# Stacked q and k loaded by six transfers on 48, 32 and 16 partitions instead of twelve on 16

## The chip, the cores and the metric

The kernel runs on one core of a Trainium2 chip. The metric is the device time of one execution in microseconds, lower is better. The core has a matrix engine (TensorE, PE in the profile, with PEld for its weight loads), VectorE (DVE), ScalarE (ACT), GpSimd (POOL) and SyncE (SP), which here only issues transfers between DRAM and the on-chip memory (SBUF, 128 partitions). Sixteen DMA engines carry the transfers. The result must equal the reference in float32.

## The reference

A transformer block of six sublayers on 4 x 1024 tokens of 256 features; attention occurs twice, after a mixture-of-experts sublayer and after a table-lookup sublayer:

```python
x = x + 0.5 * _L0_ffn_ref(_layernorm(x), ...)
x = x + _L0_attn_ref(_layernorm(x), Wq, bq, Wk, bk, Wv, bv, Wo, bo)
x = x + 0.5 * _L0_ffn_ref(_layernorm(x), ...)
x = x + 0.5 * _L1_ffn_ref(_layernorm(x), ...)
x = x + _L1_attn_ref(_layernorm(x), Wq, Wk, Wv, Wp)
x = x + 0.5 * _L1_ffn_ref(_layernorm(x), ...)
```

Both attentions have 16 heads of dimension 16, causal:

```python
q = (jnp.einsum('btc,oc->bto', x, Wq) + bq).reshape(Bb, Tt, H, D).transpose(0, 2, 1, 3)
logits = jnp.einsum('bhqd,bhkd->bhqk', q, k) / jnp.sqrt(jnp.float32(D))
attn = jax.nn.softmax(jnp.where(causal, -jnp.inf, logits), axis=-1)
out = jnp.einsum('bhqk,bhkd->bhqd', attn, v).transpose(0, 2, 1, 3).reshape(Bb, Tt, C)
y = jnp.einsum('btc,oc->bto', out, Wo) + bo
```

## The kernel before, in words

The phases run one after the other: moe0, attn0, moe1, lut0, attn1, lut1. An attention phase is a projection (`project_phase`) followed by the heads stage (`heads_phase`).

**Projection.** The weights are loaded into `w_raw` and split into a rounded part `w_hi` (ACT, L453) and a rest `w_lo` (DVE, L567), since float32 products are made of three products of rounded operands. In attn0 the biases of q and k come into `b_col` by two loads (L256), and `bv_row` by one behind them (L258); ACT waits for all of them (`b_loaded`, 48) ahead of its read of the indices of the lookup. For each tile of 512 tokens, q and k come out with their 256 features on partitions, in two halves of 128 rows. Each value is then split into three bfloat16 parts, which are stored to `q_dram` and `k_dram`, of shape (batch 4, part 3, feature 256, token 1024) in bfloat16. Row h x 16 + d of a part is dimension d of head h.

**Heads.** The stage goes over 16 quads, n = 4 x batch + quad, of four heads each. For a quad, q and k stand in `q_st` and `k_st` as stacks on 96 partitions: six blocks of 16 dimensions, with 4 heads x 1024 tokens in the free dimension, 8 KB per partition. The blocks pair the parts of q and k so that one matmul over 96 partitions sums the six products (0,0), (1,0), (2,0), (0,1), (1,1), (0,2) of parts. There are R = 3 such stacks, used in turn.

For each quad, PE computes 32 units of scores (L1008), whose row maxima DVE takes (L1180). GpSimd splits the maxima in three parts, PE turns them (L1018), DVE copies them out, and SP writes them into three more rows of the stack, 96 to 98 (`put_max`, L847, from 96 partitions to 3). Then PE computes the scores transposed over 99 rows (L1027, 48 pieces in a quad, `st_full`), ACT takes their exponential (L1118), and PE multiplies with v (L1043). PE runs the units ahead: in quad n it interleaves the units of quad n+1 from the tenth on and the first nine of quad n+2 (LEAD = 9, by the list PACE). The first unit of a quad waits for its stack's twelve transfers (`stack_loaded`, LOAD).

**SP's order around the loads.** At the start: load(0), load(1), the output weights, the bias, load(2), put_max(0). Then for each n from 0 to 15: for 1 <= n < 14 wait until the transposed scores of quad n-1 are done (`st_full`) and issue load(n+2); store(n-1, 1) and store(n, 0) of o (L843); put_max(n+1); for n = 0 three loads of x (L878); and `output_ahead(n)`, which in the first quad of a batch loads the sums and rows of the batch before (L857, L860) and x, and in the second stores the inverses (L864) and loads them spread over 16 dimensions each (`load_inv`, L872, source (8 heads, 16 repeated, 512) onto 128 partitions). All of these are transfers on one queue. `load` is L829 to L838:

```python
for at, (ql, kl) in enumerate(((0, 0), (1, 0), (2, 0), (0, 1), (1, 1), (0, 2))):
    to = slice(at * HD, (at + 1) * HD)
    sp.dma_start(q_st[to, r, :, :], q_v[ql]).then_inc(stack_loaded[r], 16)
    sp.dma_start(k_st[to, r, :, :], k_v[kl]).then_inc(stack_loaded[r], 16)
```

A view `q_v[l]` is (16 dimensions, 4 heads, 1024 tokens) with runs of 2 KB in DRAM, since the rows of one dimension of neighbouring heads lie 16 rows apart.

Of the kernel before, what the change touches and what calls it, by code (L numbers as in the profile page):

```python
# [5 lines left out]
ALU = mybir.AluOpType  # L6
ACT = mybir.ActivationFunctionType
AX = mybir.AxisListType
F32 = mybir.dt.float32
# [4 lines left out]
P = 128  # L14
TOK = 4096
D = 256
KD = D // P
# [15 lines left out]
HEADS = 16  # L33
HD = D // HEADS
SEQ = 1024
# [4 lines left out]
QUAD = P // VW  # L40
QUADS = HEADS // QUAD
SPLIT = 3
# [46 lines left out]
def project_phase(nc, name, x_in, w_qkv, b_qkv, q_dram, k_dram, v_sb, consts, combine=None, lookup=None):  # L89
# [6 lines left out]
    with ExitStack() as ctx:  # L96
        def sb(n, shape, dt=F32):
            return ctx.enter_context(nc.sbuf_tensor(f"{name}_{n}", shape, dt))
# [6 lines left out]
        def sem(n):  # L105
            sems.append(ctx.enter_context(nc.semaphore(f"{name}_{n}")))
            return sems[-1]

        w_raw = sb("w_raw", [P, 3, KD, D])
        w_hi = sb("w_hi", [P, 3, KD, D], F32R)  # L110
        w_lo = sb("w_lo", [P, 3, KD, D], F32R)
# [13 lines left out]
        if biased:  # L125
            b_col = sb("b_col", [P, 4])
# [11 lines left out]
        b_loaded = sem("b_loaded")  # L138
        w_hi_ready = sem("w_hi_ready")
# [64 lines left out]
        def x_complete(engine, t):  # L204
            engine.wait_ge(x_loaded[t % RX], 16 * (t // RX + 1))
            if combine:
                engine.wait_ge(y_used, SUB * (t + 1))

        def idx_slot(c):
            return 1 if c == CHUNKS - 1 else 0  # L210

        with nc.Block() as block:

            @block.sync
            def _(sp):
                def load_x(t):
                    if t >= RX:
                        if combine:
                            sp.wait_ge(x_stored[t % RX], 16 * (t // RX))
                        sp.wait_ge(xn_ready, t - RX + 1)  # L220
                    sp.dma_start(x_sb[:, t % RX, :, :], x_in_v[t, :, :, :]).then_inc(x_loaded[t % RX], 16)

                def load_idx(c):
                    slot = idx_int[:, idx_slot(c), :]
                    loaded = idx_loaded[idx_slot(c)]
                    gate_up = slot[:, 0:2 * D].rearrange("p (m k h) -> p m k h", m=2, k=KD)
                    if c < CHUNKS - 1:
                        if c >= 1:
                            sp.wait_ge(idx_ready, c)
                        for m in range(2):  # L230
                            sp.dma_start(gate_up[:, m, :, :], idx[m].rearrange("(k p) h -> p k h", p=P)[:, :, c * P:(c + 1) * P])\
                                .then_inc(loaded, 16)
                        sp.dma_start(slot[:, 2 * D:3 * D], idx[2][c * P:(c + 1) * P, :]).then_inc(loaded, 16)
                    else:

                        sp.wait_ge(idx_padded, 1)
                        for m in range(2):
                            sp.dma_start(gate_up[:, 0, :, m * HALF:m * HALF + TAIL],
                                         idx[m].rearrange("(k p) h -> p k h", p=P)[:, :, c * P:INTER]).then_inc(loaded, 16)
                        sp.dma_start(slot[HALF:HALF + TAIL, 2 * D:3 * D], idx[2][c * P:INTER, :]).then_inc(loaded, 16)  # L240

                def store_found(piece):
                    sp.wait_ge(found_ready, piece + 1)
                    sp.dma_start(w_dram[:, piece * TILE:(piece + 1) * TILE], found[:, piece % 2, :]).then_inc(found_stored[piece % 2], 16)

                load_x(0)
                for n, w in enumerate(w_qkv):
                    sp.dma_start(w_raw[:, n, :, :], w.rearrange("(k p) o -> p k o", p=P)).then_inc(w_loaded, 16)
                if lookup:
                    sp.dma_start(lut_row[:, :], lut.rearrange("(a n) -> a n", a=1).to_broadcast([P, LUT])).then_inc(lut_loaded, 16)  # L250
                    load_idx(0)
                for t in range(1, RX):
                    load_x(t)
                if biased:
                    for n in range(2):
                        sp.dma_start(b_col[:, 2 * n:2 * n + 2], b_qkv[n].rearrange("(m p) -> p m", p=P),  # L256
                                     allow_slow_non_contiguous=True).then_inc(b_loaded, 16)
                    sp.dma_start(bv_row[:, :], b_qkv[2].rearrange("(a d) -> a d", a=1)).then_inc(b_loaded, 16)  # L258
                if lookup:
                    load_idx(CHUNKS - 1)  # L260
                    for c in range(1, CHUNKS - 1):
                        load_idx(c)
                for t in range(TILES):
                    if combine:
                        x_complete(sp, t)
                        sp.dma_start(x_out_v[t, :, :, :], x_sb[:, t % RX, :, :]).then_inc(x_stored[t % RX], 16)
                    if lookup:
                        store_found(t)
                    for m in range(4):
                        dram = (q_dram, k_dram)[m // 2]  # L270
                        rows = slice((m % 2) * P, (m % 2 + 1) * P)
                        sp.wait_ge(parts_ready, t * 4 + m + 1)
                        sp.dma_start(dram[t // 2, :, rows, (t % 2) * TILE:(t % 2 + 1) * TILE].rearrange("l r t -> r l t"),
                                     parts[:, t % 2, m, :, :]).then_inc(qk_stored[t % 2], 16)
                        if m == 0 and t + RX < TILES:
                            load_x(t + RX)
                if lookup:
                    for piece in range(TILES, PIECES):
                        store_found(piece)
                    for r in range(2):  # L280
                        sp.wait_ge(found_stored[r], 16 * len(range(r, PIECES, 2)))
                if combine:
                    for r in range(RX):
                        sp.wait_ge(x_stored[r], 16 * len(range(r, TILES, RX)))
                for r in range(2):
                    sp.wait_ge(qk_stored[r], 64 * (TILES // 2))
# [118 lines left out]
            def _(act):  # L405
# [44 lines left out]

                for n in range(3):
                    act.wait_ge(w_loaded, 48)
                    act.activation(w_hi[:, n, :, :], w_raw[:, n, :, :], ACT.Copy).then_inc(w_hi_ready, 1)  # L453
                if biased:
                    act.wait_ge(b_loaded, 48)
                    act.activation(bv_parts[:, 0, :], bv_row[:, :], ACT.Copy).then_inc(bv_hi_ready, 1)
                if lookup:
                    for c in range(CHUNKS):
# [36 lines left out]
            def _(dve):  # L495
# [68 lines left out]
                                          ALU.mult).then_inc(diag_ready, 1)  # L564
                for n in range(3):
                    dve.wait_ge(w_hi_ready, n + 1)
                    dve.tensor_tensor(w_lo[:, n, :, :], w_raw[:, n, :, :], w_hi[:, n, :, :].bitcast(F32), ALU.subtract)\  # L567
                        .then_inc(w_ready, 1)
                for half in range(2):
                    if lookup:  # L570
# [117 lines left out]
def heads_phase(nc, name, q_dram, k_dram, v_sb, o_dram, inv_dram, x_in, x_out, w_o, b_o, consts):  # L688
# [10 lines left out]
    NR = 4  # L699
    DEPTH = 6 * HD  # L700
    ROWS = DEPTH + SPLIT
    LOAD = 12 * 16
    SB, OB = 4, 1
    UNIT_AT, TURN_AT = score_banks(NQ, SB)
    DIAGONAL = [s for s, (half, j) in enumerate(STEPS) if j * P >= half * TILE]
# [21 lines left out]
    with ExitStack() as ctx:  # L727
# [12 lines left out]
        q_st = sb("q_st", [P, R, QUAD, SEQ], BF16)  # L740
        k_st = sb("k_st", [P, R, QUAD, SEQ], BF16)
# [8 lines left out]
        w_raw = sb("w_raw", [P, KD, D])  # L750
        w_hi = sb("w_hi", [P, KD, D], F32R)
        w_lo = sb("w_lo", [P, KD, D], F32R)
# [12 lines left out]
        stack_loaded = [sem(f"stack_loaded{r}") for r in range(R)]  # L765
# [15 lines left out]
        b_loaded = sem("b_loaded")  # L781
        w_hi_ready = sem("w_hi_ready")
# [42 lines left out]
        with nc.Block() as block:  # L825

            @block.sync
            def _(sp):
                def load(n):  # L829
                    b, quad = divmod(n, QUADS)  # L830
                    r = n % R
                    rows = slice(quad * QUAD * HD, (quad + 1) * QUAD * HD)
                    q_v = [q_dram[b, l, rows, :].rearrange("(h d) t -> d h t", d=HD) for l in range(SPLIT)]
                    k_v = [k_dram[b, l, rows, :].rearrange("(h d) t -> d h t", d=HD) for l in range(SPLIT)]
                    for at, (ql, kl) in enumerate(((0, 0), (1, 0), (2, 0), (0, 1), (1, 1), (0, 2))):
                        to = slice(at * HD, (at + 1) * HD)
                        sp.dma_start(q_st[to, r, :, :], q_v[ql]).then_inc(stack_loaded[r], 16)
                        sp.dma_start(k_st[to, r, :, :], k_v[kl]).then_inc(stack_loaded[r], 16)  # L838

                def store(n, half):  # L840
                    b, quad = divmod(n, QUADS)
# [155 lines left out]
            def _(pe):  # L997
                def unit(g):
# [3 lines left out]
                    if k == 0:  # L1002
                        pe.wait_ge(stack_loaded[r], LOAD * (n // R + 1))
                    if over:
# [1550 lines left out]
```

## Time and profile before

| | us |
|---|---|
| median of 3 runs | 2983.54 |
| lowest, highest | 2978.67, 2984.82 |
| the profiled execution | 2974.38 |
| its span | 2972.6 |
| heads stage of attn0 | about 748 to 1303 |
| heads stage of attn1 | about 2178 to 2726 |

The rows further down come from the one profiled execution. PE, DVE, ACT, POOL and SP are the engines; SPq is SyncE's own queue of instructions, in which a transfer's row is its issue, not its movement. L1008 is line 1008 of the kernel. The granted clock (PEclk) is a share of TensorE's full speed of 2.4 GHz; the lower level is 1.2 GHz. A DMA share is the mean busy share of the 16 DMA engines, so one engine is 0.06. Every transfer leaves, beside its packets of data, small packets that signal its completion.

### The profile page before, as it was taken

The page shows a single profiled execution, that of the slowest core. Times are in us where ns is not written, and L with a number is a line of the kernel's source. Part 1 is how long each engine was busy: PE and PEld are TensorE (multiplying, and loading weights), DVE is VectorE, ACT ScalarE, POOL GpSimd, SP SyncE. Part 2 cuts the span into 40 slices and gives each one's busy share as a digit, 9 for nine tenths or more (in the row PEclk, how much of TensorE's full clock was granted, in tenths as well). Part 3 has the DMA queues.
Part 4 walks back from the last instruction along what each step waited for, and adds up shares of the span by engine and source line. Part 5 has one row for each costly group of instructions (what it writes and reads, how often), then busy time and mean ns, then how long its engine had stood idle before and what let it go on. Part 6 is the DMA issues. An engine that isn't in the chain of part 4 may idle for free. (4 is left out here: it accounts for less than half of the span.)

```text
span 2972.6 us, 49393 instructions
## 1 busy us (share of the span) xinstructions
PE 2472.1 (83%) x15186; PEld 1598.4 (54%) x15186; DVE 1951.5 (66%) x5464; ACT 1459.7 (49%) x3374; POOL 1131.3 (38%) x1578
## 2 busy tenths in 40 slices
PE   7965995788699889859929984996869999984998
PEld 6755994455133323348719973774623333333776
DVE  6854885576688768458728864773658877843444
ACT  3433552333277768624405542433627877772433
POOL 4774444665232222217754436650122222220000
PEclk9987997899699999979969996998969999997999
DMA  4453554454665666144435544331574656524000
GB/s 133 171 145 128 178 180 152 152 180 147 79 104 96 83 103 108 61 143 148 170 104 176 179 151 138 112 96 54 162 111 83 98 91 117 90 59 156 29 29 29
DMA packets 266560, 351.35 MB, mean 118 GB/s; under 512 B 41873, under 2 KB 196034, under 8 KB 266306
## 3 DMA queue, kind: packets, MB, share of 16 engines
q1 hardware_dynamic: 226370, 239.08, 35.2%
q0 software_dynamic: 39936, 109.11, 10.8%
q8 instruction: 132, 2.16, 0.3%
q14 instruction: 122, 1.00, 0.1%
HBM read 197.32 MB, written 149.95 MB: 117 GB/s over the span
## 5 line engine op out<-in xcount | busy, mean ns | idle before, releaser
L1180 DVE CUSTOM_DVE_ANT_0 attn_heads_masked_s<-attn_heads_s_ps,attn_heads_causal 128x768 bf16<-128x768 f32 (+7 forms) x1024 | 727.6, 754 | 214.5 <-PE attn_heads_s_ps L1008 212.8
L1118 ACT ACTIVATE attn_heads_probs<-attn_heads_st_ps 128x512 f32<-128x512 f32 (+3 forms) x1536 | 662.9, 494 | 270.2 <-PE attn_heads_st_ps L1027 256.9
L1008 PE MATMUL attn_heads_s_ps<-attn_heads_k_st,attn_heads_q_st 96*128 96x512 bf16 (+3 forms) x1536 | 410.3, 348 | 92.4 <-DMA attn_heads_k_st<-k_dram 77.7
L1027 PE MATMUL attn_heads_st_ps<-attn_heads_q_st,attn_heads_k_st 99*128 99x512 bf16 (+3 forms) x1536 | 427.2, 337 | 4.3 <-ACT attn_heads_probs L1118 3.6
L1043 PE MATMUL attn_heads_o_ps<-attn_heads_probs,attn_v_sb 128*32 128x512 f32 (+3 forms) x3072 | 335.0, 509 | 2.9 <-POOL attn_heads_probs L958 2.3
L1027 PEld LDWEIGHTS attn_heads_st_ps<-attn_heads_q_st,attn_heads_k_st 99*128 99x128 bf16 x1536 | 136.9, 98 | 350.7 <-ACT attn_heads_probs L1118 251.8
L958 POOL TENSOR_SCALAR_AFFINE_SELECT attn_heads_probs<-attn_heads_probs 128x512 f32<-128x512 f32 x256 | 163.7, 640 | 404.8 <-ACT attn_heads_probs L1118 399.7
L1463 POOL DMA_INDIRECT xs_dram<-moe_route_xn,rows_at x256 | 272.6, 1065 | 79.0 <-issue 76.4
L1008 PEld LDWEIGHTS attn_heads_s_ps<-attn_heads_k_st,attn_heads_q_st 96*128 96x128 bf16 x1536 | 137.2, 101 | 218.5 <-DMA attn_heads_k_st<-k_dram 83.0
L1958 POOL DMA_DIRECT2D ys_dram<-moe_expert_y_sb x288 | 158.0, 549 | 243.6 <-DVE moe_expert_y_sb L2076 243.6
L2032 ACT ACTIVATE moe_expert_xT_hi<-moe_expert_xT_ps 128x256 fp32r<-128x256 f32 x288 | 110.9, 385 | 196.2 <-PE moe_expert_xT_ps L1976 195.9
L1976 PE MATMUL moe_expert_xT_ps<-ident,moe_expert_x_sb 128*128 128x128 f32 x576 | 113.3, 279 | 98.6 <-DMA moe_expert_x_sb<-xs_dram 95.8
L2058 DVE TENSOR_TENSOR moe_expert_xT_lo<-moe_expert_xT_ps,moe_expert_xT_hi 128x256 fp32r<-128x256 f32 x288 | 122.3, 425 | 111.0 <-ACT moe_expert_xT_hi L2032 107.5
L1990 PE MATMUL moe_expert_gu_ps<-moe_w_hi,moe_expert_xT_hi 128*128 x576 | 189.0, 328 | 2.1 <-DVE moe_expert_xT_lo L2058 2.1
L1990 PE MATMUL moe_expert_gu_ps<-moe_w_hi,moe_expert_xT_lo 128*128 x576 | 163.7, 284 | 0.0
L1990 PE MATMUL moe_expert_gu_ps<-moe_w_lo,moe_expert_xT_hi 128*128 x576 | 163.5, 284 | 0.0
L70 POOL DMA_INDIRECT lut_y_sb<-ys_dram,rows_at x128 | 133.3, 1041 | 66.3 <-issue 36.1
L70 POOL DMA_INDIRECT attn_proj_y_sb<-ys_dram,rows_at x128 | 135.2, 1056 | 50.8 <-issue 37.1
L2341 ACT ACTIVATE lut_gate<-lut_g_ps 128x512 f32<-128x512 f32 x96 | 57.3, 597 | 194.2 <-PE lut_g_ps L2252 194.1
L2419 DVE SCALAR_TENSOR_TENSOR lut_hid<-lut_gate,lut_u_ps 128x512 f32<-128x512 f32 x80 | 54.9, 687 | 137.0 <-PE lut_u_ps L2252 132.8
L946 POOL CAST attn_heads_max_parts<-attn_heads_row_max 128x32 bf16<-128x32 f32 x32 | 6.8, 211 | 340.4 <-DVE attn_heads_row_max L1180 340.4
L368 PE MATMUL attn_proj_w_ps<-attn_proj_mask,attn_proj_diag 128*128 128x512 bf16 x432 | 109.9, 414 | 31.6 <-DVE attn_proj_mask L542 26.2
(263 smaller groups left out, 5941.8 us busy)
## 6 DMA issues: line engine op xcount, KB each, us to landing
moe_expert_x_sb<-xs_dram SPq DMA_DIRECT2D x288, 128.0 KB, 2.1
ys_dram<-moe_expert_y_sb POOLq DMA_DIRECT2D x288, 128.0 KB, 2.1
attn_heads_q_st<-q_dram SPq DMA_DIRECT2D x192, 128.0 KB, 8.7
attn_heads_k_st<-k_dram SPq DMA_DIRECT2D x192, 128.0 KB, 9.1
o_dram<-attn_heads_oT SPq DMA_DIRECT2D x64, 256.0 KB, 5.8
moe_route_w_raw<-in_L_ffn_we_dram SPq DMA_DIRECT2D x96, 128.0 KB
q_dram<-attn_proj_parts SPq DMA_DIRECT2D x32, 384.0 KB, 2.9
k_dram<-attn_proj_parts SPq DMA_DIRECT2D x32, 384.0 KB, 3.1
```

The costliest lines, as they stand in the source:

```text
L70: pool.indirect_dma_start(y_sb[:, r, k, :], None, ys_dram, bass.IndirectOffsetOnAxis(rows_at[:, u, k:k + 1], 0))\
L958: pool.affine_select(out=d, in_=d, compare_op=ALU.is_ge, fill=0.0, base=0, pattern=[[0, QUAD], [1, P]], channel_multiplier=-1).then_inc(ma ...
L1008: last = pe.matmul(s_ps[:, at + a // TILE, 0:w], q_st[0:DEPTH, r, h, i * P:(i + 1) * P], k_st[0:DEPTH, r, h, a:a + w], start=True, stop=True)
L1027: pe.matmul(st_ps[:, v % NB, 0:w], k_st[0:ROWS, n % R, h, j * P:(j + 1) * P], q_st[0:ROWS, n % R, h, first:first + w], start=True, stop=Tr ...
L1043: last = pe.matmul(o_ps[h * VW:(h + 1) * VW, use % OB, TILE - w:TILE], v_sb[:, at:at + VW], probs[:, G % NR, h, 0:w], start=(j == 0), stop ...
L1118: act.activation(probs[:, G % NR, h, 0:w], st_ps[:, v % NB, 0:w], ACT.Exp, scale=scale)\
L1180: dve.tensor_tensor_reduce(out=masked_s[:, use % 4, 0:w], in0=s_banks[:, at * TILE:at * TILE + w], in1=causal[:, SEQ - w:SEQ], scale=1.0, ...
L1463: pool.indirect_dma_start(xs_dram, bass.IndirectOffsetOnAxis(rows_at[:, n * SUB + s, k:k + 1], 0), xn[:, n % RX, s, :], None).then_inc(sca ...
L1958: pool.dma_start(ys_dram[s * P:(s + 1) * P, :], y_sb[:, s % AHEAD, :]).then_inc(y_stored[s % AHEAD], 16)
L1976: last = pe.transpose(xT_ps[:, s % 2, kd * P:(kd + 1) * P], x_sb[:, s % AHEAD, kd * P:(kd + 1) * P], ident[:, :])
L1990: last = pe.matmul(gu_ps[:, s % 2, 0:D], a, b, start=(n == 0), stop=(n == len(pairs) - 1))
L2058: dve.tensor_tensor(xT_lo[:, s % RH, :, :].rearrange("p k t -> p (k t)"), xT_ps[:, s % 2, 0:D], xT_hi[:, s % RH, :, :].rearrange("p k t -> ...
```

## The change

The rows of q and k are stored in another order. Within each half of 128 rows, row d x 8 + h is now dimension d of the h-th head of that half. To this end, the rounding of wq and wk reads the columns in that order and writes them side by side, the rest likewise, and the biases of q and k come by four loads of 128 values instead of two of 256. Wv keeps its order.

In DRAM one dimension of the four heads of a quad is then one run of 8 KB. The load of a stack is made of three transfers each for q and k: for l = 0, 1, 2 the blocks of 16 partitions that pair part l of k with parts 0 to 2 - l of q are loaded at once. The q transfer takes its 3, 2 or 1 parts from DRAM, the k transfer repeats part l 3, 2 or 1 times. They go to 48, 32 and 16 partitions. The bytes written into SBUF and the stack that results are as before but for the order of q's and k's columns, which is the same for both.

```diff
+        def in_order(w, n):
+            return w[:, n, :, :].rearrange("p k (m d h) -> p (k m) d h", d=HD, h=HEADS // KD) if n < 2 else w[:, n, :, :]
+
+        def by_dim(w, n):
+
+            return w[:, n, :, :].rearrange("p k (m h d) -> p (k m) d h", d=HD, h=HEADS // KD) if n < 2 else w[:, n, :, :]
...
-                        sp.dma_start(b_col[:, 2 * n:2 * n + 2], b_qkv[n].rearrange("(m p) -> p m", p=P),
-                                     allow_slow_non_contiguous=True).then_inc(b_loaded, 16)
+                        for m in range(KD):
+                            some = b_qkv[n][m * P:(m + 1) * P].rearrange("(h d) -> d h", d=HD)
+                            sp.dma_start(b_col[:, 2 * n + m:2 * n + m + 1], some, allow_slow_non_contiguous=True).then_inc(b_loaded, 16)
...
-                    act.activation(w_hi[:, n, :, :], w_raw[:, n, :, :], ACT.Copy).then_inc(w_hi_ready, 1)
+                    act.activation(in_order(w_hi, n), by_dim(w_raw, n), ACT.Copy).then_inc(w_hi_ready, 1)
                 if biased:
-                    act.wait_ge(b_loaded, 48)
+                    act.wait_ge(b_loaded, 80)
...
-                    dve.tensor_tensor(w_lo[:, n, :, :], w_raw[:, n, :, :], w_hi[:, n, :, :].bitcast(F32), ALU.subtract)\
+                    dve.tensor_tensor(in_order(w_lo, n), by_dim(w_raw, n), in_order(w_hi, n).bitcast(F32), ALU.subtract)\
...
-    LOAD = 12 * 16
+    LOAD = 2 * SPLIT * 16
...
-                    rows = slice(quad * QUAD * HD, (quad + 1) * QUAD * HD)
-                    q_v = [q_dram[b, l, rows, :].rearrange("(h d) t -> d h t", d=HD) for l in range(SPLIT)]
-                    k_v = [k_dram[b, l, rows, :].rearrange("(h d) t -> d h t", d=HD) for l in range(SPLIT)]
-                    for at, (ql, kl) in enumerate(((0, 0), (1, 0), (2, 0), (0, 1), (1, 1), (0, 2))):
-                        to = slice(at * HD, (at + 1) * HD)
-                        sp.dma_start(q_st[to, r, :, :], q_v[ql]).then_inc(stack_loaded[r], 16)
-                        sp.dma_start(k_st[to, r, :, :], k_v[kl]).then_inc(stack_loaded[r], 16)
+                    rows = slice(quad // 2 * P, (quad // 2 + 1) * P)
+                    q_v, k_v = (x[b, :, rows, :].rearrange("l (d q h) t -> l d q (h t)", d=HD, h=QUAD)[:, :, quad % 2, :] for x in (q_dram, k_dram))
+                    for l in range(SPLIT):
+                        at, count = sum(SPLIT - m for m in range(l)), SPLIT - l
+                        to = slice(at * HD, (at + count) * HD)
+                        sp.dma_start(q_st[to, r, :, :], q_v[0:count]).then_inc(stack_loaded[r], 16)
+                        sp.dma_start(k_st[to, r, :, :], k_v[l:l + 1].to_broadcast([count, HD, QUAD * SEQ])).then_inc(stack_loaded[r], 16)
```

## Rows read from the trace of the kernel before

**Rows 1.** The page: busy time by engine, with share of the span and instructions.

```profile
PE 2472.1 (83%) x15186; PEld 1598.4 (54%) x15186; DVE 1951.5 (66%) x5464; ACT 1459.7 (49%) x3374; POOL 1131.3 (38%) x1578
```

**Rows 2.** Busy time by stretch, quads 4 and 6 of attn0; columns on top.

```profile
core 0: us, PE busy (x) PEld busy (x) DVE busy (x) ACT busy (x) POOL busy (x), PEclk, DMA share, GB/s
898.00:925.00 27.00, 27.00 (x201) 9.53 (x193) 23.26 (x66) 21.73 (x51) 6.01 (x12) 1.00 0.55 80
952.00:989.00 37.00, 29.35 (x197) 10.06 (x193) 23.20 (x67) 21.94 (x52) 8.44 (x14) 0.86 0.63 88
```

**Rows 3.** Timeline of PE, attn0: start, us, engine, line, operation, [idle before, releaser].

```profile
763.49 1.36 PE L1008 MATMUL attn_heads_s_ps<-attn_heads_k_st,attn_heads_q_st 96*128 96x512 bf16 x4 [20.17 <-DMA attn_heads_k_st<-k_dram]
794.85 1.49 PE L1027 MATMUL attn_heads_st_ps<-attn_heads_q_st,attn_heads_k_st 99*128 99x512 bf16 x3
...
983.18 0.82 PE L1008 MATMUL attn_heads_s_ps<-attn_heads_k_st,attn_heads_q_st 96*128 96x512 bf16 x2 [7.65 <-DMA attn_heads_k_st<-k_dram]
1074.03 0.81 PE L1008 MATMUL attn_heads_s_ps<-attn_heads_k_st,attn_heads_q_st 96*128 96x512 bf16 x2 [4.48 <-DMA attn_heads_k_st<-k_dram]
```

**Rows 4.** Waits, whole span: us in total, times, longest.

```profile
PE attn_heads_s_ps L1008 <- DMA attn_heads_k_st<-k_dram: 77.7, 12, 20.4
```

**Rows 5.** DMA from 748 to 763 us, first loads: packets, MB, share of 16 engines.

```profile
q1 hardware_dynamic: 1077, 1.78, 101.1%
```

**Rows 6.** DMA from 1203 to 1215 us, 40 slices: four inv_all loads, one store.

```profile
DMA  0000233555455556445555311000000069500000
GB/s 0 0 0 0 27 68 143 198 198 212 191 198 212 198 178 191 184 184 198 205 205 205 150 75 48 27 0 0 0 0 0 0 273 410 191 0 0 0 0 0
DMA packets 688, 1.31 MB, mean 109 GB/s; under 512 B 48, under 2 KB 48, under 8 KB 688
q1 hardware_dynamic: 688, 1.31, 29.6%
```

**Rows 7.** Timeline of SP's queue: issues of loads, of put_max (L847) and load_inv (L872).

```profile
748.13 0.34 SPq L837 DMA_DIRECT2D attn_heads_q_st<-q_dram  x1
...
822.86 0.32 SPq L837 DMA_DIRECT2D attn_heads_q_st<-q_dram  x1
...
955.13 2.45 SPq L872 DMA_DIRECT2D attn_heads_inv_all<-inv_dram  x4
957.63 0.46 SPq L837 DMA_DIRECT2D attn_heads_q_st<-q_dram  x1
...
994.17 0.32 SPq L837 DMA_DIRECT2D attn_heads_q_st<-q_dram  x1
...
1084.69 0.46 SPq L837 DMA_DIRECT2D attn_heads_q_st<-q_dram  x1
...
1164.88 0.73 SPq L847 DMA_DIRECT2D attn_heads_q_st<-attn_heads_turned  x1
1170.64 0.50 SPq L837 DMA_DIRECT2D attn_heads_q_st<-q_dram  x1
1200.05 0.80 SPq L847 DMA_DIRECT2D attn_heads_q_st<-attn_heads_turned  x1
...
2251.77 0.32 SPq L837 DMA_DIRECT2D attn_heads_q_st<-q_dram  x1
...
2620.84 0.80 SPq L847 DMA_DIRECT2D attn_heads_q_st<-attn_heads_turned  x1
```

**Rows 8.** DMA from 898 to 901 us, 40 slices: one put_max alone.

```profile
DMA  0000000000000000001222221000000000000000
DMA packets 99, 0.02 MB, mean 8 GB/s; under 512 B 99, under 2 KB 99, under 8 KB 99
```

**Rows 9.** DMA issues, whole span: count, KB each, median us to landing.

```profile
attn_heads_sums<-o_dram SPq DMA_DIRECT2D x16, 32.0 KB, 2.2
```

**Rows 10.** Line 453: ns min/median/max, first and last start, forms.

```profile
L453 ACT ACTIVATE attn_proj_w_hi<-attn_proj_w_raw x6: 612/613/629, 485.5 to 2063.2; 128x512 fp32r<-128x512 f32 x6
```

**Rows 11.** Timeline of SP's queue, projection of attn0: the first bias load.

```profile
483.92 1.54 SPq L256 DMA_DIRECT2D attn_proj_b_col<-in_L_attn_bq_dram  x1
```

## The prediction

> **What bounds the kernel now.** The page comes first: PE is the busiest engine over the span, DVE next [rows 1]. The chain that ended last says nothing here: it covers the last stage (lut) and stops there. So the busy time by stretch is next. In an undisturbed quad of the heads stage PE is busy 27.00 of 27 us at the full clock; in quad 6 it is busy 29.35 of 37 us, at a granted clock of 0.86 [rows 2]. PE is the bound of a normal quad, and something else stops it in some. The timeline of PE names it: the first score matmul of a quad waits for the load of the stacks, 20.17 us at the start of the stage, then 7.65 and 4.48 us [rows 3]; over both attentions it is 12 waits, 77.7 us [rows 4]. The loads are therefore on the path already, at the edge: what makes a load shorter removes up to those 77.7 us and the slow clock behind them, and what makes it longer than now stalls every quad.
>
> The DMA answer for the first 15 us of the stage shows what a load costs. The 16 engines are busy the whole time (101.1%) and yet move only 1.78 MB, 119 GB/s [rows 5]. All 16 engines write into the same 16 partitions there. Where 16 engines write 128 partitions, a 256 KB store reaches 410 GB/s [rows 6]. The Trainium skill explains this ("SBUF — State Buffer", section "Door 1: The DMA port swizzle (why [64,N] ≈ [32,N])"): partitions reach memory through 16 ports, and 16 neighbours lie on four. The low rate in the rows agrees.
>
> **What the change does to a load.** A load stays at 12 x 128 KB = 1.573 MB. Six transfers of 384, 256 and 128 KB take the place of twelve; a run in a partition is 8 KB instead of 2 KB. SP issues six instructions fewer, 0.32 to 0.46 us each [rows 7]; that is up to 2.8 us of SP per load, but not on the path, since the engines were the limit at 119 GB/s [rows 5]. I cost it at nothing; were the engines no limit it would give at most 2.8 us a load.
>
> The decisive question is how many engines a transfer uses. Before, the outermost dimension of a load is 16 on both sides. After, the source of the 48-partition transfer is (3, 16, 4096), that of the 32-partition one (2, 16, 4096), for q over the part and for k a repeat. Two transfers of this trace have such a small outer dimension. The load of inv_all has source (8, 16, 512) with the 16 a repeat and a destination of 128 partitions: four loads and one store give 688 packets, 640 of data and 48 under 512 B. The store on 16 engines accounts for 16 of the 48, so the loads leave 8 each; and they hold half of the engines busy (slices of 4 to 5 tenths) [rows 6]. The maxima go from 96 partitions into 3: 99 packets, 96 of data and three more, with 2 tenths busy, that is 3 of 16 engines [rows 8]. So the small outer dimension of either side sets the number of engines: the new transfers should run on 3, 2 and 16 engines.
>
> The Trainium skill has the same as a rule, and it speaks against this change ("DMA: Bandwidth & Descriptors", "Why a DMA increments its semaphore by 16 and not by 1"): the count is the largest up to 16 that divides the slowest dimension of both sides, and a leading repeat of c copies confines the transfer to c engines. Both rows agree with it. By it alone the result is the same as by the rows.
>
> **Length of a load after.** Taking the engines in order, the first carries 16 partitions x 8 KB of each of the four large transfers and one partition of each of the two small ones: 66 x 8192 B = 540.7 KB, out of 1.573 MB; 13 engines carry 16 KB each. Its rate: in [rows 6] 1.31 MB took 29.6% of 16 engines over 12 us, 56.8 engine-us, so 23.1 KB per us; the store's best slice gives 410/16 = 25.6. I take 23.1, since those loads too run on part of the engines and write SBUF: 540.7/23.1 = 23.4 us. Issue and landing add about 2.1 (a 32 KB transfer lands after 2.2 us [rows 9]): a load takes 25.5 us. With 25.6 it is 23.2; for 8 KB pieces no row exists, and I go down to 20 KB per us, 29.1 us.
>
> **What that costs in a quad.** SP issues load(n+2) when quad n begins. PE first needs it about 18 us later: issue at 957.63, PE stalled from 975.53 (983.18 less 7.65) [rows 3, 7]. From the end of the stall to the next load's issue it took 11.0 and 10.7 us (983.18 to 994.17, 1074.03 to 1084.69) [rows 3, 7], mean 10.9; that holds the rest of the quad with the slow clock that follows a stall, and the put_max transfer, which lands after the load. So the period after is 25.5 + 10.9 = 36.4 us, in every quad with a load, 13 per attention. Five of these loads are issued right behind others: inv_all is issued from 955.13 on, its four parts put 4 x 32 KB on each of the first eight engines, 5.7 us at 23.1, so until about 962, where the load would have started at 958.6; 3.2 us more [rows 7]. I take 3.2 for all five (two with inv_all, three with rows, of which two with x, 2 to 4 us): 16. Sum: 13 x 36.4 + 16 = 489.2 us per attention.
>
> Before, the same 13 periods took in the first attention 1170.64 - 822.86 = 347.8 plus 35.2 for the last (put_max 1164.88 to 1200.05) = 383.0. In the second, from the same load's issue to the same put_max 2620.84 - 2251.77 = 369.1, and put_max comes 5.8 ahead of the quad's load (1164.88, 1170.64): 374.9 [rows 7]. Added: 106.2 and 114.3.
>
> At the start, three loads stand in the queue, then put_max(0) behind them, on the same three engines. 748.1 + 2.1 + 3 x 23.4 + 1.4 (output weights, bias, the maxima) = 821.8, where the first transposed scores ran at 794.85 [rows 3]: +27 us, twice. The first units begin 10 us later (25.5 instead of 15.4 after the issue), inside that 27: their 31.1 us to 794.6 would end at 804.7. Quad 0 itself (794.85 to 822.86) stays.
>
> **Small parts.** The rounding of wq and wk reads with a stride of 64 B: 613 ns on ACT per matrix [rows 10], at the start of the projection. Bounds 0 to double, four matrices: 0 to 2.5 us on ACT, and as much again on DVE behind it; I take 0, it writes the same elements once. The q and k biases come by four loads instead of two, the first of which took 1.54 us on SP [rows 11], and bv_row is issued behind them, with ACT waiting for it and the index reads behind ACT: -0.5 to +3 us, I take 1. The stores of q and k, the matmuls, the masks stay.
>
> **Sum.** 106.2 + 114.3 + 54 + 1 = 275.5. The profiled execution took 2974.4 us; 3249.9. The median of the runs shown is 9.1 above it: 3259 us.
>
> **Rivals.** (A) Faster: the outer dimension doesn't confine these transfers and all 16 engines share them. What decides is whether 48 destination partitions are split by 16, against [rows 6, 8]. Then the partitions count: 119 GB/s on 16 [rows 5], 410 on 128 [rows 6]; between them I estimate twice 119 for both 32 and 48. 2 x (1.6 + 1.1 + 1.1) = 7.6 us for 384, 256 and 128 KB instead of 13.2. A load 5.6 us shorter leaves 2.1 of the 7.65 stall and next to nothing of the others; of the 77.7 us of waits 40.6 stand at the two starts (20.2 each, [rows 3, 4]), so 37 are in quads, and about 33 go, with the slow clock behind them (a quad of 37 us against 27 for 7.65 us of stall [rows 2, 3]) about 50, and 11 at the starts: 2983.5 - 61 = 2923. (The Trainium skill's port map, section as above, puts partitions 32 to 47 on the ports of the first 16, which would make the 48-partition transfer 1.5 times as fast as one on 16, not twice.)
>
> (B) Much slower: the first and third engine write partitions 0 to 15 and 32 to 47 in step and disturb each other. For it: sixteen engines on 16 partitions are limited to 119 GB/s in all [rows 5]. Against it: eight engines at once, in blocks of 16 partitions, keep 184 to 212 GB/s, 23 to 26 each [rows 6]. Price: q and k of the 48-partition transfer put 128 KB on each engine, 5.6 us at 23.1; at half that rate all the time +11.2 us, half of the time +5.6; I take the mean, 8.4. It adds in full, since a load is already past the 18 us. Each us of load costs 13 + 3 per attention, 32 in all: +269, 3528. (The skill's port map gives this rival its reason: partitions p and p + 32 lie on one port.)
>
> (C) No effect: a load is hidden anyway. The 12 waits [rows 4] exclude it unless both changes cancel.
>
> **Chances.** Forecast 0.68, own range 3175 to 3385 (rate 25.6: -2.3 us, -74; 20: +3.6, +115). B 0.22, 3435 to 3620. A 0.08, 2900 to 2960. C 0.02. Range 3175 to 3620 leaves out A, C and the ends of the others, about 0.18. A difference within 0.2% can't be told from none: faster 0.08, same 0.01, slower 0.91 (C counts half as small loss).
>
> **What the profile after would show.** Load transfers with 51, 34 and 32 packets if pieces are 8 KB (48+3, 32+2, 16+16); DMA share near 3 tenths in the large ones, and a long tail with 2; landing near 25 us. PE waiting for the load in every quad from the second on, 6 to 8 us, a granted clock near 0.85 to 0.9, periods of 36 to 37. If the slices show 9 tenths or a load lands within 12 us, A holds; if landing is 32 or more, B. Periods of 36 with another cause of the wait (put_max, o_dram) would make the mechanism wrong though the time be right.

## The result and the profile after

| | before | after |
|---|---|---|
| median, us | 2982.18 (4 runs) | 3324.43 (4 runs) |
| lowest to highest | 2978.67 to 2984.82 | 3317.73 to 3330.85 |
| span of the profiled execution | 2972.6 | 3316.0 |
| heads stage of attn0, from the first load's issue to the next phase's | 748.1 to 1303.0: 554.9 | 747.1 to 1472.1: 725.0 |
| heads stage of attn1 | 2178.1 to 2726.3: 548.1 | 2347.4 to 3069.5: 722.1 |

The ratio is 1.1148, with a 95% interval of 1.1123 to 1.1174. The two heads stages account for 344.1 of the 343.4 us by which the span grew. The forecast was 3259 us, range 3175 to 3620.

The busy time of the page answers to [rows 1]. PE's busy time grew by 44 us only; its share fell from 83% to 76%.

```profile
span 3316.0 us, 49187 instructions
PE 2516.1 (76%) x15170; PEld 1604.9 (48%) x15186; DVE 1953.9 (59%) x5464; ACT 1462.9 (44%) x3374; POOL 1130.8 (34%) x1578
```

The waits over the whole span answer to [rows 4]: 28 waits and 351.6 us instead of 12 and 77.7. PE waits at both starts and in each of the 26 quads with a load.

```profile
PE attn_heads_s_ps L1016 <- DMA attn_heads_k_st<-k_dram: 351.6, 28, 34.4
```

The timeline of PE answers to [rows 3]; columns as there. The first row is the start of the stage, the second the first transposed scores, which now wait for the maxima's transfer. Then come two undisturbed quads, one behind the rows of o, one behind inv_all.

```profile
776.40 1.35 PE L1016 MATMUL attn_heads_s_ps<-attn_heads_k_st,attn_heads_q_st 96*128 96x512 bf16 x4 [34.12 <-DMA attn_heads_k_st<-k_dram]
820.37 1.44 PE L1035 MATMUL attn_heads_st_ps<-attn_heads_q_st,attn_heads_k_st 99*128 99x512 bf16 x3 [12.42 <-DMA attn_heads_q_st<-attn_heads_turned]
...
914.72 0.82 PE L1016 MATMUL attn_heads_s_ps<-attn_heads_k_st,attn_heads_q_st 96*128 96x512 bf16 x2 [9.43 <-DMA attn_heads_k_st<-k_dram]
950.95 0.82 PE L1016 MATMUL attn_heads_s_ps<-attn_heads_k_st,attn_heads_q_st 96*128 96x512 bf16 x2 [7.36 <-DMA attn_heads_k_st<-k_dram]
...
1034.14 0.82 PE L1016 MATMUL attn_heads_s_ps<-attn_heads_k_st,attn_heads_q_st 96*128 96x512 bf16 x2 [14.89 <-DMA attn_heads_k_st<-k_dram]
1077.86 0.82 PE L1016 MATMUL attn_heads_s_ps<-attn_heads_k_st,attn_heads_q_st 96*128 96x512 bf16 x2 [14.83 <-DMA attn_heads_k_st<-k_dram]
```

SP's queue, the issues of the loads that end those waits, and the two of put_max that close the sum of the periods; answers to [rows 7]:

```profile
747.09 0.84 SPq L845 DMA_DIRECT2D attn_heads_q_st<-q_dram  x1
...
848.33 0.74 SPq L845 DMA_DIRECT2D attn_heads_q_st<-q_dram  x1
886.82 0.73 SPq L845 DMA_DIRECT2D attn_heads_q_st<-q_dram  x1
925.12 0.72 SPq L845 DMA_DIRECT2D attn_heads_q_st<-q_dram  x1
...
1000.54 0.74 SPq L845 DMA_DIRECT2D attn_heads_q_st<-q_dram  x1
1045.16 0.75 SPq L845 DMA_DIRECT2D attn_heads_q_st<-q_dram  x1
...
1323.03 0.77 SPq L855 DMA_DIRECT2D attn_heads_q_st<-attn_heads_turned  x1
1328.78 0.76 SPq L845 DMA_DIRECT2D attn_heads_q_st<-q_dram  x1
1367.31 0.77 SPq L855 DMA_DIRECT2D attn_heads_q_st<-attn_heads_turned  x1
```

A load is issued at 886.82 and PE goes on at 914.72: 27.9 us. For the next shown it is 25.8 (925.12 to 950.95). Behind the rows it is 33.6, behind inv_all 32.7. The DMA answer for the second of these loads, 925 to 951 us in 40 slices of 0.65 us, beside [rows 5]:

```profile
DMA  0030218921174222212111211119111111111111
GB/s 0 0 38 13 76 50 252 177 25 50 50 284 170 88 60 91 76 76 88 76 76 76 88 76 72 66 66 378 73 38 50 50 63 50 50 50 50 50 41 47
DMA packets 515, 2.11 MB, mean 81 GB/s; under 512 B 72, under 2 KB 72, under 8 KB 320
```

Some 4 us after the issue, for somewhat over 1 us, nearly all 16 engines work (8 and 9 tenths), on the two small transfers, which were issued last; a store of o passes at 284 and another at 378 GB/s. Otherwise the rate is mostly 60 to 91 GB/s with 1 or 2 tenths busy (3 of 16 engines) and in the end about 50 GB/s with 1 tenth (2 of 16).

### The profile page after: what moved, and what is told of

It is laid out like the page before. It is cut to its first block and busy times, and to the rows that moved or that the text cites. A ratio compares the mean times of both kernels' runs of the same rounds, so it can differ in the third digit from the quotient of the medians.

```text
span 3316.0 us, 49187 instructions
## 1 busy us (share of the span) xinstructions
PE 2516.1 (76%) x15170; PEld 1604.9 (48%) x15186; DVE 1953.9 (59%) x5464; ACT 1462.9 (44%) x3374; POOL 1130.8 (34%) x1578
## 5 line engine op out<-in xcount | busy, mean ns | idle before, releaser
L1188 DVE CUSTOM_DVE_ANT_0 attn_heads_masked_s<-attn_heads_s_ps,attn_heads_causal 128x768 bf16<-128x768 f32 (+7 forms) x1024 | 729.8, 755 | 553.8 <-PE attn_heads_s_ps L1016 551.6
L1016 PE MATMUL attn_heads_s_ps<-attn_heads_k_st,attn_heads_q_st 96*128 96x512 bf16 (+3 forms) x1536 | 424.0, 358 | 366.4 <-DMA attn_heads_k_st<-k_dram 351.6
L1035 PE MATMUL attn_heads_st_ps<-attn_heads_q_st,attn_heads_k_st 99*128 99x512 bf16 (+3 forms) x1536 | 441.1, 347 | 30.5 <-DMA attn_heads_q_st<-attn_heads_turned 26.4
L966 POOL TENSOR_SCALAR_AFFINE_SELECT attn_heads_probs<-attn_heads_probs 128x512 f32<-128x512 f32 x256 | 163.1, 637 | 726.8 <-ACT attn_heads_probs L1126 722.1
L1051 PE MATMUL attn_heads_o_ps<-attn_heads_probs,attn_v_sb 128*32 128x512 f32 (+3 forms) x3072 | 352.4, 533 | 0.7 <-ACT attn_heads_oT L1107 0.5
L70 POOL DMA_INDIRECT lut_y_sb<-ys_dram,rows_at x128 | 133.8, 1045 | 66.5 <-issue 36.1
```

The lines of the kernel that those rows point to most:

```text
L70: pool.indirect_dma_start(y_sb[:, r, k, :], None, ys_dram, bass.IndirectOffsetOnAxis(rows_at[:, u, k:k + 1], 0))\
L966: pool.affine_select(out=d, in_=d, compare_op=ALU.is_ge, fill=0.0, base=0, pattern=[[0, QUAD], [1, P]], channel_multiplier=-1).then_inc(ma ...
L1016: last = pe.matmul(s_ps[:, at + a // TILE, 0:w], q_st[0:DEPTH, r, h, i * P:(i + 1) * P], k_st[0:DEPTH, r, h, a:a + w], start=True, stop=True)
L1035: pe.matmul(st_ps[:, v % NB, 0:w], k_st[0:ROWS, n % R, h, j * P:(j + 1) * P], q_st[0:ROWS, n % R, h, first:first + w], start=True, stop=Tr ...
L1051: last = pe.matmul(o_ps[h * VW:(h + 1) * VW, use % OB, TILE - w:TILE], v_sb[:, at:at + VW], probs[:, G % NR, h, 0:w], start=(j == 0), stop ...
L1188: dve.tensor_tensor_reduce(out=masked_s[:, use % 4, 0:w], in0=s_banks[:, at * TILE:at * TILE + w], in1=causal[:, SEQ - w:SEQ], scale=1.0, ...
```

## Experiments

The experiments ran in three groups, each on another chip, and each kernel is compared with the runs of before on its own chip: 3120 us on the first, 2974 on the second, 2973 on the third. The heads stages differ less between chips (526.3 and 523.0 us for one kernel on the first two), so their lengths are given as well, as in the table above.

### The dimension outermost

```diff
-  ...rearrange("l (d q h) t -> l d q (h t)", d=HD, h=QUAD)[:, :, quad % 2, :]
+  ...rearrange("l (d q h) t -> d l q (h t)", d=HD, h=QUAD)[:, :, quad % 2, :]
-  sp.dma_start(q_st[to, r, :, :], q_v[0:count])
-  sp.dma_start(k_st[to, r, :, :], k_v[l:l + 1].to_broadcast([count, HD, QUAD * SEQ]))
+  sp.dma_start(q_st[to, r, :, :], q_v[:, 0:count, :])
+  sp.dma_start(k_st[to, r, :, :], k_v[:, l:l + 1, :].to_broadcast([HD, count, QUAD * SEQ]))
```

> The changed kernel with the dimension outermost in both sources: (16, 3, 4096), (16, 2, 4096), (16, 1, 4096), so that a block of partitions holds the parts of one dimension side by side; bytes, pieces of 8 KB, the six transfers and their partitions stay. Theory of the engine count (the outer dimension of 3 or 2 confines a transfer to 3 or 2 engines): 96 pieces over 16 engines are 12 pieces an engine in all, the completion packets rise to 16 per transfer (6 x 16 + 192 data = 288 per load instead of 192 + 42), a load lands in 8 to 13 us, PE waits for a load at the two starts alone, and the time is 2900 to 2940 us. Rival of the pieces and of the stored order (8 KB runs, or reads of rows that lie 8 KB apart, are what is slow): the load stays above 20 us and the time near 3320. Rival of the partitions (wide transfers disturb each other's writes): between them, above 3000.

Measured: 3067.09 us against 3120.21, ratio 0.9867 [0.9806, 0.9928], heads stages 526.3 and 525.4 us. The absolute time missed the forecast band, on a chip where before took 3120 us too; the ratio is inside it. PE waited for a load 7 times, 44.8 us in all, and not at the two starts alone as expected. It ran again on a chip of the usual speed:

> The version with the dimension outermost once more, beside the one with the rows behind the load, so that both are compared with the same runs of before: ratio 0.981 to 0.993 as in the first measurement, heads stages of some 526 us each.

Measured: 2918.63 us, ratio 0.9811 [0.9789, 0.9833], heads stages 523.0 and 520.5 us. The same six transfers with the same pieces, partitions and bytes cost 11.5% or gain 1.9%, by which dimension stands first in the source. The number of packets settles what differs; here are the pages of the changed kernel and of this one:

```profile
DMA packets 243359, 351.32 MB, mean 106 GB/s; under 512 B 37105, under 2 KB 191266, under 8 KB 236962
```

```profile
DMA packets 245087, 351.33 MB, mean 120 GB/s; under 512 B 38833, under 2 KB 192994, under 8 KB 238690
```

The difference is 1728 packets, all under 512 B: 54 for each of the 32 loads. Six transfers on 16 engines leave 96 completion packets; 96 - 54 = 42 = 3 + 3 + 2 + 2 + 16 + 16. So the large transfers did run on 3 and 2 engines. One load of the second run, 876.2 to 889 us, in slices of 0.32 us:

```profile
DMA  0000908999979489989697979797993887955000
GB/s 0 0 0 0 410 0 230 384 179 154 154 102 256 77 128 205 154 128 179 102 230 179 256 154 256 154 256 154 282 128 32 77 83 115 243 173 166 26 6 0
```

Nearly all slices of the load stand at 7 to 9 tenths, most at 100 to 280 GB/s, and it is over in about 10 us. In the rival of the pieces and of the stored order the loss would have stayed; it falls. The rival of the partitions asked for more than 3000 us and falls as the main cause.

### The stored order with twelve transfers

```diff
-  LOAD = 2 * SPLIT * 16
+  LOAD = 12 * 16
...
-  for l in range(SPLIT):
-      at, count = sum(SPLIT - m for m in range(l)), SPLIT - l
-      to = slice(at * HD, (at + count) * HD)
-      sp.dma_start(q_st[to, r, :, :], q_v[0:count]).then_inc(stack_loaded[r], 16)
-      sp.dma_start(k_st[to, r, :, :], k_v[l:l + 1].to_broadcast([count, HD, QUAD * SEQ])).then_inc(stack_loaded[r], 16)
+  for at, (ql, kl) in enumerate(((0, 0), (1, 0), (2, 0), (0, 1), (1, 1), (0, 2))):
+      to = slice(at * HD, (at + 1) * HD)
+      sp.dma_start(q_st[to, r, :, :], q_v[ql]).then_inc(stack_loaded[r], 16)
+      sp.dma_start(k_st[to, r, :, :], k_v[kl]).then_inc(stack_loaded[r], 16)
```

> The changed kernel's stored order with the twelve transfers of before, each (16, 4096) onto 16 partitions, in pieces of 8 KB. Theory of the engine count: all twelve run on 16 engines and the 16 partitions limit them to some 119 GB/s as before, so the load is 13 to 15 us and the time is within 10 us of before, 2970 to 2985. Rival of the stored order and of the 8 KB pieces: the loss of some 340 us stays, wholly or for the most part. It also shows what the strided rounding of the weights and the four bias loads cost: with the same loads, what is left against before; expected 0 to 3 us.

Measured: 3132.41 us, ratio 1.0044 [1.0002, 1.0085]; heads stages 559.7 and 551.6 us, 4.8 and 3.4 longer than before. The first load lets PE start 15.4 us after its issue (823.3 to 838.67), as in the kernel before (748.1 to 763.49). The stored order and the 8 KB pieces are neither the loss nor a gain: sixteen engines on 16 partitions take as long for the same bytes in 8 KB pieces as in 2 KB pieces. The few microseconds more are at the edge of the measurement.

### Half of the change: q alone, k alone

```diff
-  LOAD = 2 * SPLIT * 16
+  LOAD = 9 * 16
...
   sp.dma_start(q_st[to, r, :, :], q_v[0:count]).then_inc(stack_loaded[r], 16)
-  sp.dma_start(k_st[to, r, :, :], k_v[l:l + 1].to_broadcast([count, HD, QUAD * SEQ])).then_inc(stack_loaded[r], 16)
+  for c in range(count):
+      sp.dma_start(k_st[(at + c) * HD:(at + c + 1) * HD, r, :, :], k_v[l]).then_inc(stack_loaded[r], 16)
```

> The changed kernel with q's three wide transfers kept, whose source takes 3, 2 or 1 parts, and k's replaced by six transfers of (16, 4096) onto 16 partitions. Theory of the engine count: the first engine carries 16 + 16 + 1 pieces of q and 6 of k, 39 instead of 66, at some 0.31 us each 12.2 us, with the share of the others' writes 14 to 18 us; completion packets per load 3 + 2 + 16 + 6 x 16 = 117. A load is then about as long as before (15.4 us), and the ratio to before is 0.99 to 1.02. Rival that it is only the repeat in k that confines: q then runs on 16 engines and k on 16, the load is at most 13 us, ratio 0.985 to 0.99, and the completion packets are 144. Rival that a wide transfer is slow in itself: the load stays above 20 us.

> The mirror of it: k's wide transfers kept, whose source repeats a part 3, 2 or 1 times, and q by six of 16 partitions. Theory of the engine count: the same 39 pieces on the first engine, so the same load and the same ratio within 0.5% as with q wide: 0.99 to 1.02. Rival that only the repeat confines: this one carries the whole loss, ratio above 1.05, and the one with q wide none.

Measured: 3115.36 us, ratio 1.0467 [1.0438, 1.0495], with q wide (the edit shown), and 3118.05 us, 1.0476 [1.0452, 1.0499], with k wide (its mirror), two runs each. The pages, q wide first:

```profile
DMA packets 245761, 351.34 MB, mean 113 GB/s; under 512 B 39506, under 2 KB 193667, under 8 KB 239363
DMA packets 245760, 351.34 MB, mean 113 GB/s; under 512 B 39505, under 2 KB 193666, under 8 KB 239362
```

That is 2401 and 2400 small packets more than in the changed kernel, 75 for each of the 32 loads, and 42 + 75 = 117, as expected; the rival of the repeat asked for 144. The two times are equal as well, so a step over the parts and a repeat confine a transfer alike, and that rival falls. The ratio missed: 1.047 instead of 0.99 to 1.02. Two rows of the q variant, SP's issue and the end of PE's wait, give a load of 20.8 us (873.0 to 893.79) where I had expected 14 to 18:

```profile
893.79 0.50 PE L1017 MATMUL attn_heads_s_ps<-attn_heads_k_st,attn_heads_q_st 96*128 96x512 bf16 x2 [2.37 <-DMA attn_heads_k_st<-k_dram]
```

The number of the third rival, that a wide transfer is slow in itself, was met as well (a load above 20 us). But with 16 as the outermost dimension transfers just as wide are not slow, so this rival falls by that experiment.

I had priced all 39 pieces of the first engine at 0.31 us, with 2 to 6 us on top for the others' writes. In the packet records of this load the engine that ends last needs 11.5 us for its first 16 pieces, which belong to the 48-partition transfer of q; most of them move while the other engines work on the small transfers of k, and take up to 1.2 us each. The 16 pieces of the 32-partition transfer take 5.0 us, 0.31 each, and the seven pieces of small transfers 2.3, 0.31 to 0.41 each. 1.5 us from the issue to the first piece, 11.5 + 5.0 + 2.3, and 0.5 from the last piece to PE make the 20.8 us. What I had priced too low is the disturbance of the first 16 pieces.

### The small transfers first

```diff
-  for l in range(SPLIT):
+  for l in (2, 0, 1):
```

> The changed kernel with the two transfers of 16 partitions issued ahead of the four large ones. In the changed kernel a quad's load took 25.8 to 28.4 us where I had forecast 25.5. Theory that the small transfers, on all 16 engines and 16 partitions, slow the first engine while it carries the large ones: ahead of them they take their 2.2 us alone, and the load stays as long or gets 1 to 2 us shorter, 3260 to 3330 us. Rival that the first engine's own pieces are the whole of it (66 pieces): no change within 10 us, whatever the order. Either way it stays above 3250: the order can't take work off the first engine.

Measured: 3464.45 us against 3120.21, ratio 1.1162 [1.1078, 1.1245], beside 1.1148 for the changed kernel; the absolute band was missed with the slower chip. Heads stages 724.5 and 719.5 us against 725.0 and 722.1. The order makes no difference in the time of the stage. But that is a balance, and neither theory holds as it was put: in attn0 the eight loads with nothing in front of them took longer, 28.6 us on average instead of 27.3, and the five behind other loads less, 30.3 instead of 32.9. This kernel's trace shows best what slows the three engines of the 48-partition transfers. From 964.6 to 967.2 us only they work, as all small pieces are done; beside it, from 947 to 949 us of the changed kernel, the last two engines:

```profile
DMA packets 18, 0.15 MB, mean 57 GB/s; under 512 B 0, under 2 KB 0, under 8 KB 0
DMA packets 14, 0.11 MB, mean 57 GB/s; under 512 B 0, under 2 KB 0, under 8 KB 0
```

Three engines move no more than two. In the packet records of the first stretch one engine takes 0.31 us for each piece, and the other two take 0.61 to 0.65 for seven of their nine, in pairs that overlap: two of the three run at about half the rate.

### The rows of o and x behind the load

The version with the dimension outermost still had five waits for a load besides the starts in its first run, four of them right behind the loads of rows and x, so these were moved.

```diff
-  if b > 1:
-      load_x(RX + t - HALVES)
-      load_x(RX + t - HALVES + 1)
...
   load(n + 2)
+  if n > QUADS and n % QUADS == 1:
+      t = (n // QUADS - 1) * HALVES
+      load_values(t)
+      load_values(t + 1)
+      if n // QUADS > 1:
+          load_x(RX + t - HALVES)
+          load_x(RX + t - HALVES + 1)
```

`load_values` is the two loads of rows (L860 before) taken out of `load_rows`; the sums stay where they were.

> The version with the dimension outermost, and the rows of o and the loads of x issued behind the next stack's load instead of ahead of it. There the remaining waits for a load within the quads are five, 9.6 us in all, four of them behind rows and x. Theory that these four come from the queue: they go, and with the slow clock behind them 10 to 18 us in all; ratio to before 0.980 to 0.985, and no wait of PE for a load but at the starts. Rival: the rows then come late for GpSimd, whose masks wait behind them, and the gain is zero or negative.

Measured: 2935.41 us, ratio 0.9861 [0.9844, 0.9878]; heads stages 547.2 and 518.5 us. PE's waits for loads are down to the two starts (35.2 us in 2), as expected. The ratio missed, and attn0 lost 24 us against the version without the move: the rival. The timeline of POOL names a transfer that I had not priced:

```profile
1056.01 2.34 POOL L998 TENSOR_TENSOR attn_v_sb<-attn_v_sb,attn_heads_b_row 128x1024 f32<-128x1024 f32 x1 [14.71 <-DMA attn_v_sb<-x]
```

It is x for the addition of the bias, not the rows: GpSimd waits 14.71 us and its masks stand behind that. Such waits were 29.8 us in two, where without the move they were 6.6 in two. attn1 has no bias and gained 2 us. With only the values moved, x staying in front:

> The version with the dimension outermost; of the transfers in front of a stack's load only the values of o go behind it, x stays in front. With x behind as well, the first attention lost 24 us against the version without the move, and its trace shows GpSimd waiting 14.7 us for x in the addition of the bias, with its masks behind that; the second attention, without that addition, gained 2 us. Theory: with x in front, GpSimd waits no longer than without the move, the heads stages are 521 to 524 and 518 to 521 us, and the ratio to before is 0.979 to 0.982, 0 to 5 us better than without the move (2919 us, 0.981). Rival: the values too are needed early, by GpSimd's normalisation in the quad after, and the first attention stays 10 us or more longer than 523.

Measured: 2908.43 us, ratio 0.9782 [0.9748, 0.9815], heads stages 516.4 and 517.1 us; PE waits for loads at the two starts only:

```profile
PE attn_heads_s_ps L1026 <- DMA attn_heads_k_st<-k_dram: 34.7, 2, 17.5
```

The stages are shorter than the 521 to 524 and 518 to 521 us that I expected; the move is worth 6.6 and 3.4 us instead of 0 to 5 in all. This version is the fastest of all that ran: 64 us, 2.2%, below the 2972.75 us of the kernel before on the same chip.

## Why the prediction was right, and where it was off

**What bounds the kernel.** Right: the heads stages gave all of the difference, and in them PE's wait for the loads.

**The number of engines.** Right, and the step that carried the forecast: 3, 2 and 16 engines, as read from the load of inv_all and from put_max [rows 6, 8]. The packets show it (42, 117 and 96 small ones a load), and the slices show 3 and then 2 engines; 3 of 16 show as 2 tenths, as in [rows 8], where I had written 3. The forecast packet counts of 51, 34 and 32 per transfer sum to 234 a load, 192 of data and 42 of completion, which agrees with the counts found. The rule of the Trainium skill that the prediction cites for it ("DMA: Bandwidth & Descriptors") held in every kernel here, for a step and for a repeat.

**The length of a load.** Too small: 25.5 us forecast. For the eight loads of attn0 with nothing in front of them it was 27.3 on average (25.8 to 28.8), and PE's waits were 7.4 to 10.3 us instead of 6 to 8. The term that was mis-sized is the uniform rate of 23.1 KB per us for 66 pieces, and it was off in two opposite ways. Undisturbed, an engine moves a piece of 8 KB in 0.31 us, 26 GB/s; 66 pieces would take 20.6 us, less than the 23.4 forecast. But the engine that ends last needed 25.3 us on average from the first piece to the last (23.5 to 27.5), so 4.7 us are disturbance. With about 1.5 us from the issue to the first piece and 0.5 from the last piece to PE, that is the 27.3.

The disturbance lies in this engine's first 32 pieces, those of the 48-partition transfers. In the load of 961.99 us, 26.4 us from first piece to last, its pieces in the 32-partition transfers took 0.31 us each, 5.0 us for each 16, and the two of the small transfers, which it moves last, 0.31 each. Two things fall together with its slow pieces. First, while the other 13 engines move the small transfers, some pieces of the large ones take up to 1.2 us. The engine that ends second loses only there: its four large transfers took 7.4, 5.0, 5.0 and 5.0 us. Then, until the engine with 34 pieces is done, pieces of that engine and of the last one take 0.35 to 0.65 us again and again, in pairs at the same time. The first costs 2.2 to 2.6 us, the second 0.3 to 3.5, by how far the last two engines end apart in five loads. No run separates the two more exactly.

**The rest of the quad.** Right: 10.9 us forecast. Measured from the end of the wait to the next issue 11.0 (875.78 to 886.82), 10.4 (914.72 to 925.12), 11.0 (950.95 to 961.99). The granted clock of these quads was as forecast, 0.86, as the row of the stretch 925 to 962 us of after shows (columns as in [rows 2]):

```profile
925.00:962.00 37.00, 29.64 (x196) 10.08 (x194) 23.30 (x68) 21.76 (x53) 8.26 (x13) 0.86 0.18 59
```

**Loads behind other loads.** Too small: 3.2 us more for each of five. In attn0 these five took 32.9 us on average, 5.6 more than the others. Their first piece started 3.9 us later than that of the others (4.0 to 6.9 us after the issue instead of 0.8 to 1.6), which is near the 3.2 forecast; the other 1.7 us were slower pieces. For the one behind inv_all, whose load is issued at 1045.16, the DMA slices show the start, from 1045 to 1061 us in slices of 0.4 us: half of the engines stay busy for eleven slices, until about 1049.4, 4.2 us after the issue as forecast, and the load's own pieces follow.

```profile
DMA  5445554555579394298520320122021202222221
GB/s 195 179 184 195 189 179 184 205 195 205 200 179 282 108 328 41 41 189 241 205 61 20 82 61 20 61 82 61 20 82 61 61 20 82 61 61 82 61 61 41
```

**The sum.** The 13 periods of attn0 took 1328.78 - 848.33 = 480.5 and 44.3 (1323.03 to 1367.31), 524.7 us, where 489.2 were forecast. 13 x 1.8 + 5 x 2.4 = 35.4 of those 35.5 us are the two terms above. In both attentions together the heads stages grew by 344.1 us against 274.5 forecast (106.2 + 114.3 + 54); the 70 us missing are about twice those 35, and 65 of them are what the median measured lies above 3259.

**The start.** Right: the transposed scores were forecast 73.7 us after the first issue (821.8 - 748.1) and came 73.3 us after it (820.37 - 747.09). From the first load's issue to that of load(3) it took 101.2 and 102.7 us instead of 74.7 and 73.6: +26.5 and +29.1 for the forecast 27. PE's first units came later than forecast, 29.3 us after the issue instead of 25.5, but that stayed inside. The three loads behind each other took 70.6 us from the first piece to the last, 70.2 forecast.

**Small parts.** The rounding of the weights had a price where I took none, inside the bound of double:

```profile
L461 ACT ACTIVATE attn_proj_w_hi<-attn_proj_w_raw x6: 612/1048/1060, 485.7 to 2233.5; 128x512 fp32r<-128x512 f32 x6
```

The median rose from 613 ns [rows 10] to 1048. It was hidden: from the first rounding to the first load of the heads stage it took 261.4 us (485.7 to 747.1) where it took 262.6 before (485.5 to 748.1). The same sum contains the two bias loads more, so the 1 us that I gave them did not show either.

**The rivals.** (A) Its condition did not hold, but its time did when the condition was made: with all transfers on 16 engines the kernel took 2919 us; I had worked out 2923 for it. That is in part luck: the sum of (A) has 7.6 us for moving a load, and the slices of that kernel show about 10. Its figure of 410 GB/s for 128 partitions was misread too: the store in [rows 6] reads 128 partitions of SBUF and writes DRAM, so it says nothing on writes into SBUF.

(B) came in small, and the forecast had no term for it. Two of the three engines of the 48-partition transfers do disturb each other, down to half the rate, as the pairs of slow pieces show. It did not cost the 8.4 us a load that (B) priced but 0.3 to 3.5, since in the changed kernel the slow pieces soon alternate with pieces of 0.31 us. That one of the two is the engine with 34 pieces, the third, fits the reason that (B) gives, engines that write 32 partitions apart in step; which of the others its partner is, the trace does not show. The measured 3324 us lie between the forecast and the 3528 of (B), nearer the forecast.

(C) fell with the 28 waits.

## What to carry to other kernels

Before merging transfers, look at the dimension that comes out as the outermost on each side: a step over three parts or a repeat of three confines the transfer to three engines, and its length is then at least the bytes of one engine, here at 26 GB/s, and more where other engines disturb it. Count completion packets in a profile to see how many engines a transfer used. If the order of the partitions within a block is free, as in a sum over the contraction, put a dimension of 16 first; here this turned a loss of 11.5% into a gain of 1.9% with the same six transfers.

## What the runs showed of the hardware that was not expected

- Transfers issued one behind the other don't share a pace. In the load at 925.12 us the two small transfers, issued last, were done on 13 engines at 930.8 us, while the last engine moved its pieces of them at 949.5 to 950.2.
- What a piece costs its engine depends on what the others do at the moment. 8 KB took 0.31 us undisturbed, in a transfer on 3 or 2 engines and, at the end of a load, in one on 16; 0.61 for two of three engines of a 48-partition transfer; 0.95 on average where 16 engines worked on 16 partitions (twelve transfers, load at 924 us).
- ACT took longer for the rounding when it read float32 with a step of 16 elements, in runs of 8: 1048 ns for 512 elements per partition instead of 613.
